# A causal mask added in 64-row halves, and new orders for the attention stage of a fused transformer block

## The chip, the cores and the metric

The kernel runs on one core of a Trainium2 chip. The metric is the device time of one launch in microseconds (us), from runs of the whole program. A profile of one further execution shows every engine: TensorE (PE; its weight loads PEld), VectorE (DVE), ScalarE (ACT), GpSimd (POOL) and SyncE (SP), which issues the transfers.

## The reference

One block on x of shape (8, 512, 256) in float32: a modulated layer norm, causal linear attention with 16 heads of 16, a gated residual, a second modulated layer norm, and a mixture of 8 experts (256 to 1024 to 256, two chosen for each token). Cut to the attention, where the change is:

```python
h = _layernorm(x, axis=-1) * (1 + ca) + sa
qkv = h @ w_qkv                                  # q, k, v: (B, N, 16, 16)
q = elu(rope(q) * SCALE) + 1.0
k = elu(rope(k) * SCALE) + 1.0
def step(carry, qkv_t):
    kv = kv + einsum('bhd,bhm->bhdm', kt, vt)
    ks = ks + kt
    denom = maximum(einsum('bhd,bhd->bh', qt, ks), 1e-06)
    out_t = einsum('bhd,bhdm->bhm', qt, kv) / denom[..., None]
x = x + ga * (out @ w_out)
```

## The kernel before

The 4096 tokens are 32 chunks of 128, four for each of the 8 sequences. The first stage passes over the chunks once. For a chunk it computes the scores k q of all pairs of its 128 tokens, head by head, sets those to zero in which the key is later than the query, multiplies by v, and adds what earlier chunks of the sequence left in a running `state`. The mask is added in PSUM: before the scores, a matmul writes -1e30 at the places of later keys (and 0 elsewhere) into the bank, the scores are accumulated onto it, and a ReLU makes them zero (the true scores are not negative).

Operands are split in a high and a low float16 part. Names in the rows: `st`, `mv`, `var`, `rstd`, `nb` are the layer norm's statistics and factors (two columns, since chunk n's first norm and chunk n-5's second one share them), `h` the normalised rows and, under the same name in the rows, those of the second norm, `hT` the first transposed and modulated, `ra`/`rb` the two products of the rotary embedding, `feat` the features of q and k, `qst`/`kst` their float16 parts stacked for the products, `qstT`/`kstT` those transposed, `amhi`/`amlo` the two parts of the masked scores (a group of 8 heads each, `sc0` and `sc1`), `den` and `attn` the denominator and the quotient, `w1hi`, `w1lo` and `w` the parts of the expert weights, which are prepared in this stage a piece a chunk, `am` (from `wo`) the output projection's weight times the gate, `x` (also `x1`) the rows after the residual.

The order on each engine is written in five tables, `ORDER_PE`, `ORDER_DVE`, `ORDER_POOL`, `ORDER_ACT` and `ORDER_SP`. An entry is a piece of work and its lag: in step n the engine goes through its table and does each piece for chunk n - lag. The engines are tied only by semaphores, so a step begins on each at its own time. Within an engine the order is fixed: a piece that waits holds up everything behind it. The names of the pieces, by engine, with the lines of the function that does them:

- VectorE: `st`, `st2` (L432), `mv`, `mv2` (L438), `ve` (L445, `var`), `f` (L505, `feat`, both inputs in SBUF), `sl0`, `sl1` (L511, `amlo`, one input in PSUM), `nb` (L452, both inputs in SBUF, 2 numbers a partition), `rope` (L495, L498), `x1` (L547), `stl` (L520, `state`; not done for the fourth chunk of a sequence), `hTe` (L475), `wlo` (L558, two instructions, both inputs in SBUF), `den`, `rec`, `vlo`, `at`.
- GpSimd: `shk` (L822), `rs` (L789, `rstd`, needs `ve` and is needed by `nb`), `slo` (L829, L831; needs `shk` and ScalarE's `shq`), `R` (L836, `ra`, needs `rope`), `xm2` and `h2` (both L797), `wb` (L808, `am`, once in four steps).
- TensorE: `sc0`, `sc1` (L1127 the mask, L1135 the scores; `sc1` needs VectorE's `sl0`, `sc0` needs `sl1`), `pj` (L1189 on `am`, `aT`), `aT`, `hT`, `h2T` (L1180), `Tk`, `Tq` (L1172), `v`, `qk` (L1189), `pv0`, `pv1` (L1164 to L1166), `ear` (L1149), `state` (L1235), `lg` (L1263).
- ScalarE: `exp` (L968, L969, needs `R`), `sh0`, `sh1` (L994), `shq` (L932, `qst`), `xn`, `xn2` (L941, need `nb`), `whi`, and the copies out of PSUM (L932).

The score matmuls have 64 rows: the even head of a pair lies on partitions 0 to 63 and goes to bank 5, the odd one on 64 to 127 and goes to bank 6. The mask's matmuls have 128 rows, an identity as weights and the mask, repeated four times, as the 512 columns that pass.

## Time and profile before

| | |
|---|---|
| median of 3 runs | 819.3 us (819.18 to 821.68) |
| profiled execution | 825.53 us, span 823.2 us |
| granted TensorE clock, mean | 0.958 |
| busy: PE, DVE, ACT, POOL | 737.3, 663.8, 580.3, 514.3 us |
| attention stage | about 0 to 380 us of the span |
| routing, then the experts | about 380 to 420, then 420 to 823 us |

Busy times are sums over the span; a matmul's end is modelled, and neighbouring instructions overlap a little. A row's second number is how long its instructions lasted from the first start to the last end; what an instruction holds its engine up by is the distance to the next start.

### The profile page before, as it was taken

The numbers are of one execution on the slowest core, as the hardware profiler recorded it, in microseconds if no ns is written. First come the engines' busy times: TensorE is split into PE (matmuls) and PEld (weight loads), VectorE is DVE, ScalarE is ACT, GpSimd is POOL, SyncE is SP. The second block draws the span as 40 slices with busy tenths as digits, with TensorE's granted clock in tenths as the row PEclk, the third lists the DMA queues.
The fourth block names the chain that finished last, engine by engine and source line by source line (L and its number), as shares of the span: only waits on it lengthen the run. The fifth ranks groups of instructions, "written<-read, shape, count | busy, mean of one in ns | idle before, by whom it ended". The sixth has DMA issues, their size and how long they took to land.

```text
span 823.2 us, 26404 instructions
## 1 busy us (share of the span) xinstructions
PE 737.3 (90%) x7949; PEld 540.3 (66%) x7949; DVE 663.8 (81%) x1488; ACT 580.3 (71%) x1103; POOL 514.3 (62%) x504
## 2 busy tenths in 40 slices
PE   6599999999999999973489999999999999999994
...
GB/s 207 86 41 126 107 115 111 107 108 105 111 113 114 109 116 115 112 53 32 21 79 75 73 71 69 68 78 70 73 73 76 66 69 78 66 76 70 74 31 0
DMA packets 52814, 68.78 MB, mean 84 GB/s; under 512 B 8864, under 2 KB 44080, under 8 KB 52736
## 3 DMA queue, kind: packets, MB, share of 16 engines
...
q14 instruction: 20, 0.16, 0.1%
...
## 4 chain that ended last, share of the span: by engine, by line
PE 59%; DVE 16%; issue 10%; ACT 8%; POOL 3%; DMA 1%; DVEq 1%; another core or an unknown queue 0%; ACTq 0%; SPq 0%; POOLq 0%
PE hidden L1334 15%; PE bank L1350 15%; PE hidden L1336 8%; PE bank L1352 7%; PE bank L1189 5%; PE hidden L1172 3%; DVE amlo L511 2%; DVE nb L452 2%; PE bank L1172 2%; ACT feat L969 2%; ACT rb L968 2%; DVE rb L498 2%; DVE hT L475 2%; DVE st L432 2%; ACT qstT L932 1%
## 5 line engine op out<-in xcount | busy, mean ns | idle before, releaser
L1334 PE MATMUL hidden<-qstT,w1hi_k 128*128 128x256 f16 x1136 | 200.2, 274 | 1.1 <-DVE am L723 1.1
L1336 PE MATMUL hidden<-qstT,w1lo_k 128*128 128x128 f16 x1136 | 195.5, 220 | 0.0
L1350 PE MATMUL bank<-w,amhi 128*128 x568 | 188.6, 379 | 0.4
L1352 PE MATMUL bank<-w,amlo 128*128 x568 | 154.8, 273 | 0.0
L729 DVE TENSOR_TENSOR amlo<-am,amhi 128x512 f16<-128x512 f32 x142 | 98.4, 693 | 62.6 <-ACT am L1064 50.8
L919 POOL DMA_INDIRECT out_dram<-x,si x71 | 121.9, 1717 | 36.5 <-issue 27.4
L1334 PEld LDWEIGHTS hidden<-qstT,w1hi_k 128*128 x1136 | 111.7, 98 | 14.9 <-issue 1.3
L1336 PEld LDWEIGHTS hidden<-qstT,w1lo_k 128*128 x1136 | 111.7, 98 | 1.1
L1189 PE MATMUL bank<-wq,hT 128*128 128x256 f32 (+1 forms) x256 | 102.9, 528 | 9.2 <-DVE hT L475 9.1
L1063 ACT ACTIVATE amhi<-am 128x512 f16<-128x512 f32 x142 | 88.5, 623 | 12.6 <-DVE am L723 7.6
L1350 PEld LDWEIGHTS bank<-w,amhi 128*128 128x128 f16 x568 | 55.5, 98 | 62.3 <-issue 2.6
L1064 ACT ACTIVATE am<-am 128x512 f32<-128x512 f32 x142 | 87.5, 616 | 0.0
L900 POOL DMA_INDIRECT wq<-shares,gi x71 | 67.8, 955 | 22.1 <-issue 14.9
L511 DVE SCALAR_TENSOR_TENSOR amlo<-hidden,amhi 128x1024 f16<-128x1024 f32 x64 | 78.1, 1220 | 2.6 <-ACT amhi L994 2.3
L822 POOL CAST kst<-feat 128x512 f16<-128x512 f32 x32 | 19.5, 609 | 96.9 <-DVE feat L505 96.7
L932 ACT ACTIVATE feat<-hidden 128x512 f32<-128x512 f32 x71 | 42.4, 597 | 40.6 <-PE hidden L1336 36.3
L932 ACT ACTIVATE rb<-hidden 128x512 f32<-128x512 f32 x71 | 42.5, 598 | 38.8 <-PE hidden L1336 37.7
L1189 PEld LDWEIGHTS bank<-wq,hT 128*128 128x128 f32 x256 | 45.6, 198 | 36.3 <-issue 15.9
L994 ACT ACTIVATE amhi<-hidden 128x1024 f16<-128x1024 f32 x64 | 65.0, 1015 | 3.0 <-PE hidden L1135 1.5
L892 POOL DMA_INDIRECT xt<-ffn_rows,gi x36 | 40.4, 1122 | 41.2 <-DVE x L709 38.6
L892 POOL DMA_INDIRECT stage<-ffn_rows,gi x35 | 38.2, 1092 | 42.2 <-DVE x L709 30.7
L1352 PEld LDWEIGHTS bank<-w,amlo 128*128 128x128 f16 x568 | 55.6, 98 | 5.6
...
## 6 DMA issues: line engine op xcount, KB each, us to landing
...
```

The source lines that it names most:

```text
L511: v.scalar_tensor_tensor(out=amlo[:, g, :, :], in0=hidden[1][:, :, :], scalar=0.0, in1=amhi[:, g, :, :], op0=ALU.max, op1=ALU.subtract)\
L729: v.tensor_tensor(glo[:, a.p, h_], g32[:, a.p, h_], ghi[:, a.p, h_], ALU.subtract)\
L892: g.indirect_dma_start(xg[q], None, rows_d, bass.IndirectOffsetOnAxis(ap=gi[:, q, 0:1], axis=0)).then_inc(s_g[q], 16)
L919: g.indirect_dma_start(out_rows, bass.IndirectOffsetOnAxis(ap=si[:, m.c % GB:m.c % GB + 1], axis=0), yw[:, m.p, :], None, bounds_check=T - ...
L932: return v.activation(out_, in_, ACT.Copy, scale=scale)
L1063: v.activation(ghi[:, a.p, h_], g32[:, a.p, h_], ACT.Gelu, scale=1.0 / WS)
L1064: v.activation(g32[:, a.p, h_], g32[:, a.p, h_], ACT.Gelu, scale=1.0 / WS)\
L1189: last = t.matmul(dst, xT_[:, k * P:(k + 1) * P], w[k][:, lo], start=(k == 0), stop=(k == KT - 1))
L1334: t.matmul(dst.rearrange("p (q n) -> p q n", q=2), w1s[0][k][g][:, w_], both, start=(k == 0), stop=False)
L1336: last = t.matmul(dst[:, P:2 * P], w1s[1][k][g][:, w_], both[:, 0, :], start=False, stop=(k == KT - 1))
L1350: t.matmul(y[:, :], ghi[:, m.p, c_m], w2s[mt // 2][:, bass.ds(w_, 2 * D)], start=(mt == 0), stop=False)
L1352: last = t.matmul(y[:, D:2 * D], glo[:, m.p, c_m], w2s[mt // 2][:, bass.ds(w_, D)], start=False, stop=(mt == MT - 1))
```

## The change

Two things are changed. The mask of a bank is added by matmuls of 64 rows instead of 128: for queries 0 to 63 of the chunk and for 64 to 127 apart, with `mask_row` as weights and `later` as what passes, 256 columns each; the odd bank's use partitions 64 to 127. Queries of the first half must not see any key of the second half, which one row of ones times a row of -1e30 says. The constants for it take more instructions on GpSimd. And the five tables are written anew; the lags of `so` (4 to 6) and `ld` (1 to 0) on SyncE change too.

```diff
-ORDER_PE = (("aT", 4), ("ear", 3), ("pj", 4), ("sc1", 3), ("hT", 0), ("pv0", 3), ("Tk", 2), ("h2T", 6), ("v", 0),
-            ("Tq", 2), ("lg", 6), ("pv1", 3), ("state", 2), ("sc0", 2), ("qk", 0))
...
-ORDER_ACT = (("exp", 2), ("sh0", 3), ("shq", 2), ("sth", 3), ("aTe", 4), ("whi", 1), ("xn", 0), ("xn2", 5),
-             ("sh1", 3), ("kTs", 2), ("h2Te", 6), ("vhi", 0), ("qTs", 2), ("lge", 6))
-ORDER_SP = (("ldx", 0), ("ld", 1), ("ro", 6), ("modgb", 6), ("gb", 6), ("modg", 6), ("modb", 7), ("so", 4))
+ORDER_PE = (("aT", 4), ("ear", 3), ("sc1", 3), ("pj", 4), ("hT", 0), ("h2T", 6), ("Tk", 2), ("pv0", 3), ("v", 0),
+            ("Tq", 2), ("pv1", 3), ("lg", 6), ("state", 2), ("sc0", 2), ("qk", 0))
...
+ORDER_ACT = (("exp", 2), ("sh0", 3), ("shq", 2), ("sth", 3), ("aTe", 4), ("xn", 0), ("sh1", 3), ("whi", 1),
+             ("kTs", 2), ("xn2", 5), ("vhi", 0), ("h2Te", 6), ("qTs", 2), ("lge", 6))
+ORDER_SP = (("ldx", 0), ("modg", 6), ("modb", 7), ("so", 6), ("ro", 6), ("ld", 0), ("modgb", 6), ("gb", 6))
...
-        ident_b = sb("ident_b", [P, P], BF16)
-        later = sb("later", [P, P], BF16)
+        mask_row = sb("mask_row", [P, 2, P], BF16)
+        later = sb("later", [P, 2, P // 2], BF16)
...
-        POOL_CONST = 16
+        POOL_CONST = 26
...
+                half = P // 2
+                for u in range(2):
+                    r = slice(u * half, (u + 1) * half)
+                    for late_q in range(2):
+                        link(g.affine_select(out=mask_row[r, late_q, :], in_=mask_row[r, late_q, :],
+                                             compare_op=ALU.not_equal, fill=1.0, base=-half * late_q,
+                                             pattern=[[1, P]], channel_multiplier=-1))
+                    link(g.affine_select(out=later[r, :, :], in_=later[r, :, :], compare_op=ALU.is_ge, fill=MASKED,
+                                         base=0, pattern=[[0, 2], [1, half]], channel_multiplier=-1))
+                    link(g.memset(mask_row[u * half:u * half + 1, 0, 0:half], 0.0))
+                    link(g.memset(mask_row[u * half:u * half + 1, 0, half:P], 1.0))
+                    link(g.memset(later[u * half:u * half + 1, 0, :], MASKED))
...
-                for odd in range(2):
-                    t.matmul(bank[5 + odd].rearrange("p (h t) -> p h t", t=P), ident_b[:, :],
-                             later[:, :].rearrange("p (u t) -> p u t", u=1).broadcast_to([P, 4, P]),
-                             start=True, stop=False, skip_group_check=True)
+                half = P // 2
+                for late_q in range(2):
+                    for odd in range(2):
+                        r = slice(odd * half, (odd + 1) * half)
+                        t.matmul(bank[5 + odd].rearrange("p (h t) -> p h t", t=P)[:, :, late_q * half:(late_q + 1) * half],
+                                 mask_row[r, late_q, :],
+                                 later[r, late_q, :].rearrange("p (u t) -> p u t", u=1).broadcast_to([half, 4, half]),
+                                 start=(late_q == 0), stop=False, skip_group_check=True)
```

The first place is VectorE at the beginning of a step (here the first one whose code is in the loop over sequences), before:

```order
L505 SCALAR_TENSOR_TENSOR feat<-feat,rb 128x512
...
L432 BN_STATS st<-xt 128x6
...
L432 BN_STATS st<-x 128x6
...
L438 BN_AGGR mv<-st 128x2 x2
...
L445 TENSOR_SCALAR var<-mv 128x2
...
L511 SCALAR_TENSOR_TENSOR amlo<-hidden,amhi 128x1024
...
L452 SCALAR_TENSOR_TENSOR nb<-mv,rstd 128x2
```

and now:

```order
L432 BN_STATS st<-x 128x6
...
L432 BN_STATS st<-xt 128x6
L438 BN_AGGR mv<-st 128x2
...
L438 BN_AGGR mv<-st 128x2
...
L445 TENSOR_SCALAR var<-mv 128x2
...
L505 SCALAR_TENSOR_TENSOR feat<-feat,rb 128x512
...
L511 SCALAR_TENSOR_TENSOR amlo<-hidden,amhi 128x1024
...
L452 SCALAR_TENSOR_TENSOR nb<-mv,rstd 128x2
```

`feat` moves from ahead of the statistics to behind `var`, between what `rstd` waits for and the scores. Later in the step `state` now comes before `x`, and `v` before `den`.

The second place is GpSimd in a step in which `am` is made (the seventh step), before:

```order
L822 CAST kst<-feat 128x16x32
L789 TENSOR_TENSOR rstd<-var,minus_half 128x2
L829 TENSOR_TENSOR qst<-feat,qst 128x32x16
L831 TENSOR_TENSOR kst<-feat,kst 128x16x32
L836 TENSOR_TENSOR ra<-ra,rb 128x512
L797 TENSOR_TENSOR h<-h,mod_b 128x256 x2
L808 TENSOR_TENSOR am<-wo,am 128x512
```

and now (the lines are 10 further down in the changed file):

```order
L799 TENSOR_TENSOR rstd<-var,minus_half 128x2
L832 CAST kst<-feat 128x16x32
L839 TENSOR_TENSOR qst<-feat,qst 128x32x16
L841 TENSOR_TENSOR kst<-feat,kst 128x16x32
L818 TENSOR_TENSOR am<-wo,am 128x512
L846 TENSOR_TENSOR ra<-ra,rb 128x512
L807 TENSOR_TENSOR h<-h,mod_b 128x256 x2
```

`rstd` moves ahead of the cast, and `am` from the end to ahead of `ra`.

The third place is TensorE around the second half of the scores, in a step early in the program, before:

```order
L1180 MATMUL bank<-ident,attn 128x128 x2
L1189 MATMUL bank<-am,aT 128x256 x2
L1127 MATMUL hidden<-later,ident_b 128x512 x2
L1135 MATMUL hidden<-qstT,kstT 128x128 x8
L1180 MATMUL bank<-ident,h 128x128 x2
```

and now:

```order
L1194 MATMUL bank<-ident,attn 128x128 x2
L1140 MATMUL hidden<-later,mask_row 128x4x64 x4
L1149 MATMUL hidden<-qstT,kstT 128x128 x8
L1203 MATMUL bank<-am,aT 128x256 x2
L1194 MATMUL bank<-ident,h 128x128 x4
```

The projection (`pj`, on `am` and `aT`) moves behind the scores, and the mask is four matmuls instead of two.

## Rows read from the trace of the kernel before

**Rows 1.** Windows, 100 to 140 us: busy us (instructions) by engine, clock, DMA.

```profile
100.00:140.00 40.00, 36.90 (x505) 25.27 (x501) 38.30 (x85) 34.70 (x64) 25.92 (x28) 1.00 0.36 114
```

**Rows 2.** Source lines L505, L452: duration ns min/median/max, first and last start.

```profile
L505 DVE SCALAR_TENSOR_TENSOR feat<-feat,rb x32: 691/692/694, 27.6 to 353.0; 128x512 f32<-128x512 f32 x32
...
L452 DVE SCALAR_TENSOR_TENSOR nb<-mv,rstd x37: 149/900/1104, 6.4 to 375.2; 128x2 f32<-128x2 f32 x37
```

**Rows 3.** Timeline of VectorE, one step: start, us, instruction [idle before].

```profile
217.50 0.69 DVE L505 SCALAR_TENSOR_TENSOR feat<-feat,rb 128x512 f32<-128x512 f32 x1
...
219.23 0.17 DVE L445 TENSOR_SCALAR var<-mv 128x2 f32<-128x2 f32 x1
219.33 1.23 DVE L511 SCALAR_TENSOR_TENSOR amlo<-hidden,amhi 128x1024 f16<-128x1024 f32 x1
220.47 0.93 DVE L452 SCALAR_TENSOR_TENSOR nb<-mv,rstd 128x2 f32<-128x2 f32 x1
221.33 0.68 DVE L495 TENSOR_TENSOR ra<-bank,cos_t 128x512 f32<-128x512 f32 x1
...
222.86 0.60 DVE L520 TENSOR_TENSOR state<-hidden,state 64x136 f16<-64x136 f32 x2
...
225.26 1.52 DVE L558 SCALAR_TENSOR_TENSOR w<-stage,w 128x512 f32 x2
...
228.13 0.69 DVE L505 SCALAR_TENSOR_TENSOR feat<-feat,rb 128x512 f32<-128x512 f32 x1 [0.16 <-ACT feat L969]
```

**Rows 4.** Timeline of GpSimd, the same step.

```profile
218.53 0.61 POOL L822 CAST kst<-feat 128x512 f16<-128x512 f32 x1 [3.45 <-DVE feat L505]
219.56 0.70 POOL L789 TENSOR_TENSOR rstd<-var,minus_half 128x2 f32<-128x2 f32 x1 [0.42 <-DVE var L445]
220.23 1.16 POOL L829 TENSOR_TENSOR qst<-feat,qst 128x512 f16<-128x512 f32 x1
...
222.68 1.27 POOL L836 TENSOR_TENSOR ra<-ra,rb 128x512 f32<-128x512 f32 x1 [0.18 <-DVE rb L498]
223.91 0.73 POOL L797 TENSOR_TENSOR h<-h,mod_b 128x256 f32<-128x256 f32 x1
224.90 0.73 POOL L797 TENSOR_TENSOR h<-h,mod_b 128x256 f32<-128x256 f32 x1 [0.26 <-POOL h L797]
```

**Rows 5.** Source line L558, 100 to 330 us.

```profile
L558 DVE SCALAR_TENSOR_TENSOR w1lo_k<-stage,w1hi_k x23: 677/683/1220, 109.7 to 329.8; 128x512 f32 x20, 128x512 f16<-128x512 f32 x3
```

**Rows 6.** Timeline of VectorE and GpSimd, another step.

```profile
119.71 1.82 DVE L558 SCALAR_TENSOR_TENSOR w1lo_k<-stage,w1hi_k 128x512 f32 x2
...
119.75 1.23 POOL L797 TENSOR_TENSOR h<-h,mod_b 128x256 f32<-128x256 f32 x1 [0.18 <-POOL h L797]
120.94 1.73 POOL L808 TENSOR_TENSOR am<-wo,am 128x512 f32 x1
```

**Rows 7.** Timeline of TensorE, the step of rows 3.

```profile
220.23 1.13 PE L1189 MATMUL bank<-am,aT 128*128 x4 [0.21 <-ACT aT L932]
221.19 0.59 PE L1127 MATMUL hidden<-later,ident_b 128*128 128x512 bf16 x2
221.72 0.40 PE L1135 MATMUL hidden<-qstT,kstT 64*128 64x128 f16 x8
222.31 0.44 PE L1180 MATMUL bank<-ident,h 128*128 128x128 f32 x2 [0.20 <-ACT h L941]
...
223.20 0.61 PE L1172 MATMUL hidden<-ident,kst 128*128 128x128 f16 x8
```

**Rows 8.** Timeline of ScalarE, the step of rows 3 and the next.

```profile
221.65 0.60 ACT L941 ACTIVATE h<-xt,nb,rstd 128x256 f32 x1 [0.57 <-DVE nb L452]
...
229.00 0.62 ACT L932 ACTIVATE qst<-feat 128x512 f16<-128x512 f32 x1
```

**Rows 9.** Timeline of GpSimd at the start.

```profile
6.34 0.20 POOL L752 MEMSET ones<- 128x128 f16 x1
...
14.99 0.70 POOL L789 TENSOR_TENSOR rstd<-var,minus_half 128x2 f32<-128x2 f32 x1 [3.82 <-DVE var L445]
```

More of the change, by code:

```diff
@@ L58 @@
 Q_SCALE = WS * float(HD ** -0.25)
-ORDER_PE = (("aT", 4), ("ear", 3), ("pj", 4), ("sc1", 3), ("hT", 0), ("pv0", 3), ("Tk", 2), ("h2T", 6), ("v", 0),
-            ("Tq", 2), ("lg", 6), ("pv1", 3), ("state", 2), ("sc0", 2), ("qk", 0))
-ORDER_DVE = (("f", 2), ("st", 0), ("st2", 5), ("mv", 0), ("mv2", 5), ("ve", 0), ("sl0", 3), ("nb", 0), ("rope", 1),
-             ("x1", 4), ("stl", 3), ("hTe", 0), ("sl1", 3), ("wlo", 1), ("den", 3), ("rec", 3), ("vlo", 0), ("at", 3))
-ORDER_POOL = (("shk", 2), ("rs", 0), ("slo", 2), ("R", 1), ("xm2", 5), ("h2", 5), ("wb", 2))
-ORDER_ACT = (("exp", 2), ("sh0", 3), ("shq", 2), ("sth", 3), ("aTe", 4), ("whi", 1), ("xn", 0), ("xn2", 5),
-             ("sh1", 3), ("kTs", 2), ("h2Te", 6), ("vhi", 0), ("qTs", 2), ("lge", 6))
-ORDER_SP = (("ldx", 0), ("ld", 1), ("ro", 6), ("modgb", 6), ("gb", 6), ("modg", 6), ("modb", 7), ("so", 4))
+ORDER_PE = (("aT", 4), ("ear", 3), ("sc1", 3), ("pj", 4), ("hT", 0), ("h2T", 6), ("Tk", 2), ("pv0", 3), ("v", 0),
+            ("Tq", 2), ("pv1", 3), ("lg", 6), ("state", 2), ("sc0", 2), ("qk", 0))
+ORDER_DVE = (("st2", 5), ("st", 0), ("mv2", 5), ("mv", 0), ("ve", 0), ("f", 2), ("sl0", 3), ("nb", 0), ("rope", 1),
+             ("stl", 3), ("x1", 4), ("hTe", 0), ("sl1", 3), ("wlo", 1), ("vlo", 0), ("den", 3), ("rec", 3), ("at", 3))
+ORDER_POOL = (("rs", 0), ("shk", 2), ("slo", 2), ("wb", 2), ("R", 1), ("xm2", 5), ("h2", 5))
+ORDER_ACT = (("exp", 2), ("sh0", 3), ("shq", 2), ("sth", 3), ("aTe", 4), ("xn", 0), ("sh1", 3), ("whi", 1),
+             ("kTs", 2), ("xn2", 5), ("vhi", 0), ("h2Te", 6), ("qTs", 2), ("lge", 6))
+ORDER_SP = (("ldx", 0), ("modg", 6), ("modb", 7), ("so", 6), ("ro", 6), ("ld", 0), ("modgb", 6), ("gb", 6))
 NORM2 = 5
@@ L384, in carry @@
             eng.sem_inc(s_carry, 1)
-        POOL_CONST = 16
-        POOL_TWO, POOL_EROW = 37, 50
+        POOL_CONST = 26
+        POOL_TWO, POOL_EROW = 47, 60
         POOL_IDENT, POOL_FIRST = 2, 4
@@ L753, in attention_constants @@
                 link(g.memset(ident16[:, :], 0.0))
-                link(g.memset(ident_b[:, :], 0.0))
-                link(g.memset(later[:, :], 0.0))
+                link(g.memset(mask_row[:, :, :], 0.0))
+                link(g.memset(later[:, :, :], 0.0))
                 link(g.memset(v16[:, :, 0, :, HD:VW], 1.0))
@@ L758, in attention_constants @@
                 link(g.memset(state[:, :, :, :], 0.0))
-                for t in (ident16, ident_b):
-                    diagonal(t)
-                for t, fill in ((upto, 0.0), (later, MASKED)):
-                    link(g.affine_select(out=t[:, :], in_=t[:, :], compare_op=ALU.is_ge, fill=fill, base=0,
-                                         pattern=[[1, P]], channel_multiplier=-1))
+                diagonal(ident16)
+                link(g.affine_select(out=upto[:, :], in_=upto[:, :], compare_op=ALU.is_ge, fill=0.0, base=0,
+                                     pattern=[[1, P]], channel_multiplier=-1))
[5 more added lines that the diff above has]
+                                             compare_op=ALU.not_equal, fill=1.0, base=-half * late_q,
+                                             pattern=[[1, P]], channel_multiplier=-1))
+                    link(g.affine_select(out=later[r, :, :], in_=later[r, :, :], compare_op=ALU.is_ge, fill=MASKED,
[3 more added lines that the diff above has]
+                    link(g.memset(later[u * half:u * half + 1, 0, :], MASKED))
                 assert link.n == POOL_CONST, link.n
```

## The prediction

> **What bounds the kernel now.** I first read the windows: from 100 to 140 us VectorE is busy 38.3 of 40 us, TensorE 36.9, ScalarE 34.7, GpSimd 25.9, at a granted clock of 1.00 (the level of 2.4 GHz) [rows 1]. Only VectorE has almost no idle time there. The row on `feat` gives the step: 32 starts of L505 from 27.6 to 353.0 us, so 325.4 / 31 = 10.50 us a step [rows 2]. The second stage (from 420 us) and the routing between them are not touched.
>
> Then I read one step of VectorE in order of time, from 217.50 to 228.13, 10.63 us [rows 3]. It is a chain without holes, but `nb` (L452), which works on two numbers a partition, lasts 0.93 us and holds the next start back by 0.86 (220.47 to 221.33). Free, it takes 0.149; its median is 0.900 [rows 2]. GpSimd's `qst` (L829) runs from 220.23 to 221.39 [rows 4]: `nb` ends when that does, at 221.40. The same meeting is seen at L558 (two SBUF inputs too): 0.677 us at best, 1.220 at most [rows 5]. In [rows 6] the pair of L558 takes 1.82 instead of 1.36 and the GpSimd addition beside it 1.23 instead of 0.73: first the addition waits for the first piece, then the second piece for the addition. Operations of VectorE with an input in PSUM show nothing of this: GpSimd's next one, `kst` (L831), fills the time to 222.50 (the row of `ra` at 222.68 has only 0.18 us idle ahead of it [rows 4]), and L495 starts at 221.33 and takes 0.68 beside it [rows 3].
>
> So VectorE's own work in this step is 10.63 less 0.71 (`nb`), 0.16 (L558: 1.52 for 1.36) and 0.16 (`feat` waited for ScalarE) = 9.60 us. What keeps it at 10.5 is mainly the meeting of `nb` with `qst`. TensorE has some 0.8 us of idle time a step (3.1 of 40 us), ScalarE 1.4: both become bounds not far below 9.6.
>
> The Trainium skill (SBUF — State Buffer, Who interferes with whom) says that a VectorE instruction with two SBUF inputs contends with a GpSimd instruction that reads SBUF, that who comes first holds the pair of ports for the whole instruction, and that the order of issue decides who blocks. The rows above agree (0.93 against 0.149). By that rule a new order moves waits rather than removing them; where to, the next part works out from rows.
>
> **The new order, step by step.** I take 0 as the start of VectorE's first statistics in a step, and keep the distances between starts of [rows 3].
>
> VectorE: four statistics and `var` come first now; in [rows 3] `var` is 1.73 behind `feat`, of which `feat` is 0.61, so `var` stands at 1.12. `feat` starts at about 1.20 and ends at 1.89; the scores (L511) start at 1.81 and end at 3.04; `nb` comes up at 2.95 (L511 keeps the next start back 1.14).
>
> GpSimd: `rstd` now stands ahead of `kst`'s cast. It could start 0.16 behind `var`, at 1.45, but `feat` holds the reads to 1.89. In [rows 6] an addition of 0.73 ends 0.59 after the piece that blocked it, so 0.14 of an operation is ahead of the lock; `rstd` (0.70, [rows 4]) ends at 1.89 + 0.56 = 2.45. The cast runs 2.42 to 3.03. `nb` comes up at 2.95: it waits under 0.1 us for the cast. ScalarE's `qst` copy (0.62, 0.18 behind `feat`'s end: 228.82 to 229.00 [rows 8]) is done about 2.7, so L829 starts near 3.0, when `nb` already stands in line. **`nb` costs 0.05 to 0.2 instead of 0.86: 0.7 us saved**, in each of the steps.
>
> Behind it GpSimd has `qst` 3.0 to 4.16, `kst` (1.11 behind it now, 221.39 to 222.50) to 5.28, then `ra` (L836) to 6.5, the multiplication of `h` (L797) 6.5 to 7.2, the addition 7.46 to 8.2: starts at the distances of [rows 4]. The weights' low part (L558) is on VectorE 7.76 behind `feat` now [rows 3]; with `nb` 0.7 shorter and the same work ahead of it, it comes up at 7.05. Its first piece waits for the multiplication's end (to 7.2, of which 0.14 is start-up: nothing), runs to 7.8; the addition has stood in line since 7.46, takes its turn to 8.35; the second piece, up at 7.75, waits and ends near 8.9. Free, it would end at 8.4. **The lock costs 0.5 us there, where it costs 0.16 in the step of rows 3**. So the step is 9.60 + 0.05 + 0.45 = 10.1 us.
>
> In one step of four `am` (L808, 1.73 us [rows 6]) is made. It moves from behind `h` to ahead of `ra`. The same step has no `state` (L520, 0.60 [rows 3]), so L558 is 0.6 earlier. It meets `ra` (1.27): its second piece waits some 1.1 us. That step: 9.60 - 0.6 + 1.2 = 10.2. `ra` is done at 8.7; the next `feat` stands at 10.1 + 1.2 = 11.3, and between them are two operations of ScalarE of about the size of its `qst` copy, so `feat` doesn't wait. The routing constants and `am` also stand ahead of `ra` once at the start: under 1 us.
>
> **The mask.** Before, two matmuls of 512 columns over 128 rows: the first scores start 0.53 after the mask, 221.19 to 221.72 [rows 7]. Of this two streams of 0.213 are columns; about 0.1 is the change to matmuls of 64 rows. After, four of 256 columns over 64 rows each, odd and even in turns. Eight matmuls of 128 columns over 128 rows (L1172) take 0.61 from first start to last end, the eight of the scores, over 64 rows, 0.40 [rows 7]: 30 ns less for each of seven distances, of which the columns are 53 ns at 2.4 GHz. So halves run in pairs, and the mask's four should take 0.21 instead of 0.43; the bounds are nothing saved (they don't pair) and 0.32 (the switch vanishes too). I take 0.22, twice a step. The switch stands ahead of the mask now, and there are as many. The Trainium skill (TensorEngine Tiling, Key Properties) says that tiles work independently and that changing the mode drains the engine; by it the sum would be the same.
>
> These 0.44 us a step are on no bound: TensorE has idle time. They matter in one place. `sc1` now comes before `pj`, and `x` (L547) needs `pj`. From the end of the scores' subtraction: old mask 0.53, scores 0.33, `pj` 1.13 [rows 7] and 0.1 of latency = 2.1 us; VectorE meanwhile does `nb`, rope and `state`: 0.1, 1.53 (221.33 to 222.86, less 0.33 for `x`, which stands there now) and 0.6 [rows 3], about 1.95. With the old mask `x` would wait 0.1 us, and 0.7 in the step without `state`: 0.25 on average. The new mask takes this off nearly whole, so I count 0. `hT`, behind `pj` (0.96 between starts, then 0.44), is ready at about 5.0; L475 comes up at 3.1 + 1.53 + 0.6 = 5.2, behind rope, `state` and `x`; ScalarE's `h` follows `nb` by 0.25 as now (221.40 to 221.65 [rows 8]) and is no later than `pj`.
>
> **The start.** GpSimd's constants run from 6.34 to 11.17 (`rstd` at 14.99 has 3.82 us idle ahead of it [rows 9]), 12 instructions at 0.4 us in the mean. Ten more, net, mostly smaller, are about 3 us and at most 4: they end at 14.2 to 15.2, in the hole or 0.2 beyond it.
>
> **Queues.** SyncE now loads a weight piece a step earlier relative to its use and stores `x1` two steps later, behind waits of its own; a load of `xt` or of a piece has about a step between its issue and its use. I count nothing; were that cover gone, a late one would hold VectorE or ScalarE up by what it lacks, which no row here shows.
>
> **Sum.** Now 10.50 a step; then (3 x 10.1 + 10.2) / 4 = 10.12. Saved 0.38 x 31 = 11.8, less 0.5 for the start: 11.3 us. The profiled execution would go from 825.5 to 814.2, the median of runs from 819.3 to **808.0** (the profiled one is 6.2 above it).
>
> **Rivals.**
> A. The meeting at L558 doesn't happen, because GpSimd's addition falls before or behind it. For: in most steps now it doesn't (half the L558 take under 0.683 [rows 5]), and the new order may settle so. Against: by my times they overlap by half a microsecond. The step is 9.7, a saving of 0.8 x 31 = 25: 794 us. Chance 0.16.
> B. No change: the lock's price at L558 and small waits for `pj`, `hT` or ScalarE come to 0.8 us a step instead of 0.45. For: TensorE and ScalarE have only 0.8 and 1.4 us. Against: the mask gives TensorE 0.44. 817 to 822 us. Chance 0.13.
> C. Slower: L558 meets both the multiplication and the addition in full, each 0.59 of lock: 1.18, so 9.7 + 1.18 = 10.88, 0.38 x 31 = 12 more: 831 us. It decides from 0.8 us of waiting a step on. For: VectorE and GpSimd are tied by their waits, so the meeting, once there, repeats in each step, as `nb`'s does now. Against: it needs L558 0.6 us earlier than I have it. Chance 0.11.
> The forecast itself (L558 loses 0.3 to 0.7 us): 0.60, 801 to 815.
>
> **Range and chances.** About 0.3% is what a measurement can tell from no change, 816.8 to 821.8. Faster: forecast and A, 0.76; same: 0.13; slower: 0.11. For 8 in 10 I take 795 to 821: it leaves out C and the lower half of A.
>
> **What would show it.** Right: `nb` near 0.2 to 0.3 us in the median; L558's mean above 0.9; starts of `feat` 10.1 us apart; the scores 0.3 us behind the mask's first matmul; VectorE again with no idle time. Wrong: `nb` still 0.9 (`feat` or the cast come late, then `qst` is ahead of `nb` again); VectorE waiting for `pj` or for scores (then TensorE's order is the bound); or L558's mean unchanged (A) or above 1.2 (C).

## The result and the profile after

The changed kernel takes 811.5 us (median of 4 executions, 809.99 to 811.72); the kernel before, on the same chip, takes 820.5 us (4 executions, 819.18 to 821.68). The ratio is 0.989, with a 95% interval of 0.986 to 0.991: 9.0 us less by the medians, where 11.3 were forecast. The time lies within the forecast's own 801 to 815. One execution is left out of all that follows, of the run e6 below: it took 3306 us, the other five 805.1 to 807.7.

The profiled execution took 809.99 us, its span is 807.9. The same stretch of windows as in [rows 1], columns as there:

```profile
100.00:140.00 40.00, 36.02 (x533) 27.89 (x529) 36.98 (x86) 35.81 (x67) 28.91 (x29) 1.00 0.39 120
```

VectorE (third figure) has gone from 38.3 to 37.0 busy us of 40 although more operations fit in: it now has 3.0 us of idle time. ScalarE has 35.8 instead of 34.7. The clock is at its upper level, as before. The source lines of `feat`, `nb` and the low parts (L558; these from 100 to 330 us), to be held against [rows 2, 5] (duration ns min/median/max, first and last start):

```profile
L505 DVE SCALAR_TENSOR_TENSOR feat<-feat,rb x32: 683/685/793, 28.7 to 341.9; 128x512 f32<-128x512 f32 x32
L452 DVE SCALAR_TENSOR_TENSOR nb<-mv,rstd x37: 147/150/1129, 6.4 to 364.5; 128x2 f32<-128x2 f32 x37
L558 DVE SCALAR_TENSOR_TENSOR w1lo_k<-stage,w1hi_k x24: 679/948/1420, 107.7 to 319.6; 128x512 f32 x20, 128x512 f16<-128x512 f32 x4
L558 DVE SCALAR_TENSOR_TENSOR w<-stage,w x22: 678/681/685, 128.1 to 329.5; 128x512 f32 x18, 128x512 f16<-128x512 f32 x4
```

[rows 5] has the pieces of L558 that write `w1lo_k`; those that write `w` took, before:

```profile
L558 DVE SCALAR_TENSOR_TENSOR w<-stage,w x21: 676/680/1150, 99.9 to 310.1; 128x512 f32 x19, 128x512 f16<-128x512 f32 x2
```

From the first `feat` to the last it is now 341.9 - 28.7 = 313.2 us, 10.10 a step, against 325.4 and 10.50 [rows 2]: 12.2 us saved there, 11.8 were forecast. The first `feat` starts 1.1 us later, which leaves 11.1 at the last one. Behind the last `feat` the two profiled executions differ by another 4 us (span less last start: 470.2 and 466.0), 3.5 of it in the experts: from the first start of L729 to the last it is 386.3 and 382.7 us. The change doesn't touch that stage, and of the runs below e10 to e12 take 385.8 to 386.5 there and the others 382.3 to 382.9, whatever their orders: that belongs to the executions. `nb` is at 0.150 in the median instead of 0.900.

VectorE, one step and the end of the next:

```profile
222.16 0.41 DVE L438 BATCH_NORM_AGGREGATE mv<-st 128x2 f32<-128x6 f32 x2
222.78 0.17 DVE L445 TENSOR_SCALAR var<-mv 128x2 f32<-128x2 f32 x1 [0.21 <-DVE mv L438]
222.86 0.68 DVE L505 SCALAR_TENSOR_TENSOR feat<-feat,rb 128x512 f32<-128x512 f32 x1
223.46 1.22 DVE L511 SCALAR_TENSOR_TENSOR amlo<-hidden,amhi 128x1024 f16<-128x1024 f32 x1
224.59 0.15 DVE L452 SCALAR_TENSOR_TENSOR nb<-mv,rstd 128x2 f32<-128x2 f32 x1
224.66 0.68 DVE L495 TENSOR_TENSOR ra<-bank,cos_t 128x512 f32<-128x512 f32 x1
225.26 0.68 DVE L498 TENSOR_TENSOR rb<-bank,sin_t 128x512 f32<-128x512 f32 x1
225.86 0.60 DVE L520 TENSOR_TENSOR state<-hidden,state 64x136 f16<-64x136 f32 x2
226.70 0.42 DVE L547 TENSOR_TENSOR x<-bank,xt 128x256 f32<-128x256 f32 x1 [0.24 <-PE bank L1203]
227.04 0.72 DVE L475 TENSOR_SCALAR hT<-bank,mod_t 128x128 f32<-128x128 f32 x2
227.68 1.21 DVE L511 SCALAR_TENSOR_TENSOR amlo<-hidden,amhi 128x1024 f16<-128x1024 f32 x1
228.81 1.28 DVE L558 SCALAR_TENSOR_TENSOR w1lo_k<-stage,w1hi_k 128x512 f32 x2
...
232.62 0.68 DVE L505 SCALAR_TENSOR_TENSOR feat<-feat,rb 128x512 f32<-128x512 f32 x1
...
236.52 0.42 DVE L547 TENSOR_TENSOR x<-bank,xt 128x256 f32<-128x256 f32 x1 [0.82 <-PE bank L1203]
...
238.63 2.37 DVE L558 SCALAR_TENSOR_TENSOR w1lo_k<-stage,w1hi_k 128x512 f32 x2
```

GpSimd, the same two steps:

```profile
223.11 0.99 POOL L799 TENSOR_TENSOR rstd<-var,minus_half 128x2 f32<-128x2 f32 x1 [1.11 <-DVE var L445]
224.05 0.61 POOL L832 CAST kst<-feat 128x512 f16<-128x512 f32 x1
224.81 1.16 POOL L839 TENSOR_TENSOR qst<-feat,qst 128x512 f16<-128x512 f32 x1 [0.15 <-POOL kst L832]
...
229.73 0.96 POOL L807 TENSOR_TENSOR h<-h,mod_b 128x256 f32<-128x256 f32 x1 [1.39 <-ACT h L951]
...
236.82 1.27 POOL L818 TENSOR_TENSOR am<-wo,am 128x512 f32 x1
238.04 1.28 POOL L846 TENSOR_TENSOR ra<-ra,rb 128x512 f32<-128x512 f32 x1
239.28 1.18 POOL L807 TENSOR_TENSOR h<-h,mod_b 128x256 f32<-128x256 f32 x1
```

Read them side by side. `nb` (224.59) is done before `qst` starts (224.81): the order of the two has turned round, as forecast. `rstd` starts at 223.11, while `feat` holds the reads, and takes 0.99 instead of 0.70. The low parts (228.81) run free at 1.28, since the multiplication of `h` now comes behind their start, at 229.73: it waited 1.39 for ScalarE's `h`. In the step with `am`, `ra` comes late (238.04) and the pair takes 2.37. And `x` (L547), which never waited in [rows 3], waits for the projection's matmuls, 0.24 us here and 0.82 in the step without `state`. A second new wait, 0.21 us ahead of `var` (L445), is put down to VectorE's own `mv`; it comes in three steps of four, and what causes it was not tried.

TensorE, at the second scores of this step, for [rows 7]:

```profile
224.73 0.39 PE L1140 MATMUL hidden<-later,mask_row 64*128 64x256 bf16 x4 [0.32 <-DVE amlo L511]
224.96 0.39 PE L1149 MATMUL hidden<-qstT,kstT 64*128 64x128 f16 x8
225.28 1.13 PE L1203 MATMUL bank<-am,aT 128*128 x4
```

From the mask's first matmul to the first scores it is 0.23 us, where it was 0.53. `pj` starts 0.55 behind the mask and `x` 1.42 behind `pj`. So the path is: scores' subtraction ends (224.68), mask, scores, `pj`, `x`.

### The profile page after: what moved, and what is told of

Same layout as the page of the kernel before. It is cut to its first block, busy times and chain, and to the rows that moved or that the text cites. A ratio compares the mean times of both kernels' runs of the same rounds, so it can differ in the third digit from the quotient of the medians.

```text
span 807.9 us, 26660 instructions
## 1 busy us (share of the span) xinstructions
PE 716.7 (89%) x8077; PEld 548.9 (68%) x8077; DVE 642.3 (80%) x1488; ACT 573.0 (71%) x1103; POOL 540.8 (67%) x514
## 4 chain that ended last, share of the span: by engine, by line
PE 54%; DVE 20%; issue 12%; POOL 8%; ACT 2%; DVEq 1%; DMA 1%; POOLq 0%; SPq 0%; ACTq 0%
PE hidden L1348 16%; PE bank L1364 15%; PE hidden L1350 8%; PE bank L1366 7%; DVE amlo L511 3%; PE bank L1203 3%; DVE w1lo_k L558 2%; PE bank L1186 2%; DVE st L432 1%; DVE hT L475 1%; POOL mod_b L880 1%; DVE rb L498 1%; POOL rstd L799 1%; POOL qst L839 1%; POOL kst L841 1%
## 5 line engine op out<-in xcount | busy, mean ns | idle before, releaser
L1348 PE MATMUL hidden<-qstT,w1hi_k 128*128 128x256 f16 x1136 | 198.1, 273 | 0.0
L929 POOL DMA_INDIRECT out_dram<-x,si x71 | 129.2, 1820 | 38.3 <-issue 22.1
L729 DVE TENSOR_TENSOR amlo<-am,amhi 128x512 f16<-128x512 f32 x142 | 98.3, 692 | 51.3 <-ACT am L1074 48.2
L807 POOL TENSOR_TENSOR h<-h,mod_b 128x256 f32<-128x256 f32 x64 | 59.7, 933 | 42.7 <-ACT h L951 36.1
L910 POOL DMA_INDIRECT wq<-shares,gi x71 | 68.2, 961 | 22.1 <-DMA out_dram<-x,si 14.6
L799 POOL TENSOR_TENSOR rstd<-var,minus_half 128x2 f32<-128x2 f32 x37 | 35.8, 968 | 66.2 <-DVE var L445 66.1
L511 DVE SCALAR_TENSOR_TENSOR amlo<-hidden,amhi 128x1024 f16<-128x1024 f32 x64 | 77.8, 1216 | 1.0 <-ACT amhi L1004 0.7
L723 DVE TENSOR_TENSOR am<-hidden,rb 128x512 f32<-128x512 f32 x71 | 49.1, 691 | 29.0 <-ACT rb L942 28.9
```

What stands on the lines that cost most here:

```text
L511: v.scalar_tensor_tensor(out=amlo[:, g, :, :], in0=hidden[1][:, :, :], scalar=0.0, in1=amhi[:, g, :, :], op0=ALU.max, op1=ALU.subtract)\
L729: v.tensor_tensor(glo[:, a.p, h_], g32[:, a.p, h_], ghi[:, a.p, h_], ALU.subtract)\
L929: g.indirect_dma_start(out_rows, bass.IndirectOffsetOnAxis(ap=si[:, m.c % GB:m.c % GB + 1], axis=0), yw[:, m.p, :], None, bounds_check=T - ...
L1348: t.matmul(dst.rearrange("p (q n) -> p q n", q=2), w1s[0][k][g][:, w_], both, start=(k == 0), stop=False)
```

## The experiments

Two theories stood at the start, called L and M in the expectations. L is the prediction's: the orders free `nb` and bring the gain, the mask's matmuls are on no bound. M: the faster mask made the gain, the orders little. What the runs left standing is neither: what `nb` gives back comes again as other waits, and the mask's time is on the path of one of them. Every ratio is to the kernel before on the same chip; its medians were 821.1, 820.6, 825.6 and 822.0 us in the four sets (e1 to e4; e5 to e9; e10 to e12; e13). "Step" is the mean distance of the 32 starts of `feat`.

### The change taken apart: e1_old_mask and e2_mask_only

e1 has all the new orders and the old mask:

```diff
-                        t.matmul(bank[5 + odd].rearrange("p (h t) -> p h t", t=P)[:, :, late_q * half:(late_q + 1) * half],
-                                 mask_row[r, late_q, :],
...
+                    t.matmul(bank[5 + odd].rearrange("p (h t) -> p h t", t=P), ident_b[:, :],
+                             later[:, :].rearrange("p (u t) -> p u t", u=1).broadcast_to([P, 4, P]),
+                             start=True, stop=False, skip_group_check=True)
```

Expected: 

> The kernel before with the five new order tables and the old mask (two matmuls of 512 columns over 128 rows). Theory L (the gain is the meeting of nb with a GpSimd read that is gone): VectorE's nb again takes 0.15 us, and nearly all of the gain is there; only x waits longer for pj behind the slower mask, up to 0.3 us a step, so 812 to 818 us, ratio 0.990 to 0.998. Theory M (the faster mask made the gain, the orders little): 819 to 822 us, ratio 1.00, although nb takes 0.15.

Measured: 824.5 us, ratio 1.004 (1.002 to 1.005); step 10.52. VectorE and TensorE of e1:

```profile
222.12 0.15 DVE L452 SCALAR_TENSOR_TENSOR nb<-mv,rstd 128x2 f32<-128x2 f32 x1
...
224.67 0.42 DVE L547 TENSOR_TENSOR x<-bank,xt 128x256 f32<-128x256 f32 x1 [0.68 <-PE bank L1189]
...
226.85 1.82 DVE L558 SCALAR_TENSOR_TENSOR w<-stage,w 128x512 f32 x2
```

```profile
222.27 0.60 PE L1127 MATMUL hidden<-later,ident_b 128*128 128x512 bf16 x2 [1.00 <-DVE amlo L511]
222.80 0.40 PE L1135 MATMUL hidden<-qstT,kstT 64*128 64x128 f16 x8
223.13 1.13 PE L1189 MATMUL bank<-am,aT 128*128 x4
```

`nb` is free here too, and nothing is gained: L's 812 to 818 us is missed, and the time is a little above M's 819 to 822. Mask to scores is 0.53, mask to `pj` 0.86, which is 0.31 more than after, and `x` waits 0.57, 0.67, 0.56 and 1.15 us in the four kinds of step instead of 0.24, 0.35, 0.24 and 0.82: 0.33 more in each. Being later, the low parts meet GpSimd's `h` again (1.82 instead of 1.28) in two steps of four.

e2 has the new mask in the old orders (the diff of e1 the other way round, on the kernel before).

Expected: 

> The kernel before with the new mask alone (four matmuls of 256 columns over 64 rows), the old orders. Theory L: TensorE has idle time and VectorE doesn't, so nothing: 819 to 821 us, ratio 0.998 to 1.001, nb's median still 0.9 us, the distance from the mask's first matmul to the scores 0.23 us instead of 0.53. Theory M: 0.6 us less on TensorE in each of 32 steps is most of the gain: 811 to 815 us.

Measured: 822.8 us, ratio 1.002 (1.000 to 1.003); step 10.48, `nb` still 0.9. TensorE is busy 35.2 of 40 us from 100 to 140 us instead of 36.9: the time is off TensorE, but it was nobody's wait. That is against M, which asked for 811 to 815. So neither part brings anything alone, and the two together bring 1.1%.

### One wait removed by two moves: e3_two_swaps

The kernel before, with `f` behind `ve` and `rs` ahead of `shk`:

```diff
-ORDER_DVE = (("f", 2), ("st", 0), ("st2", 5), ("mv", 0), ("mv2", 5), ("ve", 0), ("sl0", 3), ("nb", 0), ("rope", 1),
+ORDER_DVE = (("st", 0), ("st2", 5), ("mv", 0), ("mv2", 5), ("ve", 0), ("f", 2), ("sl0", 3), ("nb", 0), ("rope", 1),
-ORDER_POOL = (("shk", 2), ("rs", 0), ("slo", 2), ("R", 1), ("xm2", 5), ("h2", 5), ("wb", 2))
+ORDER_POOL = (("rs", 0), ("shk", 2), ("slo", 2), ("R", 1), ("xm2", 5), ("h2", 5), ("wb", 2))
```

Expected: 

> The kernel before (old mask) with two moves alone: feat (f) behind var on VectorE, rstd (rs) ahead of the cast (shk) on GpSimd. Theory L: these two moves are what frees nb; its median falls from 0.9 to 0.15 us, and the step from 10.5 to 9.9 to 10.2 us, so 808 to 815 us, unless feat, now 1.2 us later, makes the scores' operands late. Theory M or a theory that the other moves matter as much: 818 us or more.

Measured: 825.2 us, ratio 1.004 (1.003 to 1.006); step 10.51. `nb` takes 0.15. ScalarE, TensorE and VectorE of e3:

```profile
228.40 0.63 ACT L932 ACTIVATE qst<-feat 128x512 f16<-128x512 f32 x1 [0.68 <-DVE feat L505]
228.94 0.57 ACT L932 ACTIVATE state<-hidden 64x136 f16<-64x136 f32 x2
229.53 0.38 ACT L932 ACTIVATE aT<-bank 128x256 f32<-128x256 f32 x1
```

```profile
229.97 1.13 PE L1189 MATMUL bank<-am,aT 128*128 x4 [0.78 <-ACT aT L932]
```

```profile
231.39 0.42 DVE L547 TENSOR_TENSOR x<-bank,xt 128x256 f32<-128x256 f32 x1 [0.61 <-PE bank L1189]
```

The wait has moved: `feat` is later, ScalarE's `qst` copy waits for it (0.68), `aT` stands behind that in ScalarE's order, `pj` waits for `aT` (0.78) and `x` for `pj` (0.61). The 0.7 us of `nb` went to `x`, which waits 0.62, 0.87 and 0.62 us in three kinds of step; in the one with `am`, `hT` waits 0.56 for TensorE. The 808 to 815 us expected are missed: these two moves free `nb` and are no gain without others.

### The lock by itself: e4_nb_one_input

The kernel before with `nb` written as two instructions that have one tensor input in SBUF each; `rstd` comes in as the scalar of each partition. Same values, same orders, old mask.

```diff
-                v.scalar_tensor_tensor(out=nb[:, :], in0=mv[:, :, 0], scalar=-1.0, in1=rstd[:, :],
-                                       op0=ALU.mult, op1=ALU.mult).then_inc(a_["nb"], 1)
+                for k in range(2):
+                    last = v.tensor_scalar(nb[:, k:k + 1], mv[:, k, 0:1], rstd[:, k:k + 1], -1.0, ALU.mult, ALU.mult)
+                last.then_inc(a_["nb"], 1)
```

Expected: 

> The kernel before with the same orders and mask, but nb is made by two instructions of one column each, which have one tensor input (mv) and take rstd as a scalar for each partition, instead of one with two SBUF tensor inputs. Theory L in its strict form (what blocks is the second SBUF tensor input): the two take 0.15 us each and start without waiting for GpSimd's qst, 0.25 us for the pair instead of 0.86, a saving of 0.6 us a step, 804 to 812 us (ratio about 0.985). Rival: any VectorE instruction that starts beside a GpSimd one on small tensors, or the wait for rstd, is what holds it up: nb still ends when qst does, 819 to 824 us.

Measured: 807.6 us, ratio 0.983 (0.981 to 0.985); step 9.98. GpSimd and VectorE of e4:

```profile
220.30 1.17 POOL L830 TENSOR_TENSOR qst<-feat,qst 128x512 f16<-128x512 f32 x1
```

```profile
220.51 0.33 DVE L453 TENSOR_SCALAR nb<-mv,rstd 128x1 f32<-128x1 f32 x2
220.75 0.68 DVE L496 TENSOR_TENSOR ra<-bank,cos_t 128x512 f32<-128x512 f32 x1
...
224.69 1.82 DVE L559 SCALAR_TENSOR_TENSOR w1lo_k<-stage,w1hi_k 128x512 f32 x2
```

`nb` stands in the middle of `qst`, exactly where it took 0.9, and takes 0.33 for both columns. That shows the cause of its 0.9: the second tensor input in SBUF, not its place as such. The instruction's kind, which e4 changes too, is not it: L511 is a SCALAR_TENSOR_TENSOR with one input in PSUM, and in [rows 3] it takes 1.23 us beside GpSimd's `rstd` (219.56), where its mean is 1.22. The Trainium skill (SBUF — State Buffer, Who interferes with whom) says that a VectorE instruction with at most one SBUF input, outside the modes in which it uses both ports, doesn't contend with GpSimd; this run agrees (0.33 for the two, in the middle of `qst`). Part of what `nb` gave back was lost at L559 (L558 before), whose pair takes 1.82 in most steps where it took about 1.5. And this edit of three lines gains more than the change does.

### The mask's order: e5_no_pairs

The changed kernel with the two loops of the mask exchanged, so that a row group's two matmuls follow each other:

```diff
-                for late_q in range(2):
-                    for odd in range(2):
+                for odd in range(2):
+                    for late_q in range(2):
```

Expected: 

> The changed kernel, with the mask's four matmuls in another order: both of the even bank (rows 0 to 63), then both of the odd bank, so that neighbours use the same rows of the array. If matmuls on different rows run in pairs, this undoes the pairing: the first scores start 0.4 to 0.45 us behind the mask's first matmul instead of 0.23, and since the old mask on these orders cost 1.5% at 0.53, this costs about two thirds of that: 818 to 822 us. If the pairing is not what shortened the mask (but that no change of row mode lies between mask and scores), it stays at 0.23 to 0.3 and 811 us.

Measured: 812.7 us, ratio 0.990 (0.988 to 0.992); step 10.12. TensorE of e5:

```profile
225.28 0.40 PE L1140 MATMUL hidden<-later,mask_row 64*128 64x256 bf16 x4 [0.32 <-DVE amlo L511]
225.50 0.39 PE L1149 MATMUL hidden<-qstT,kstT 64*128 64x128 f16 x8
225.82 1.13 PE L1203 MATMUL bank<-am,aT 128*128 x4
```

0.22 to the scores and 0.54 to `pj`: as after. The order within the mask doesn't matter. The 818 to 822 us expected of matmuls that can no longer pair are missed. But they still pair: mask and scores are 4 x 256 + 8 x 128 = 2048 columns in 0.54 us, which one behind the other at the rate of the wide ones (0.213 us for 512, as in the prediction) would take 0.85; and of the mask's four, two start within 0.01 us of each other and the other two, as close together, 0.12 later, in e5 as after. Which row group each of them belongs to, the trace doesn't tell.

### Where `am` is made: e6_wb_last and e12_old_mask_wb_last

The changed kernel with `wb` back at the end of GpSimd's order:

```diff
-ORDER_POOL = (("rs", 0), ("shk", 2), ("slo", 2), ("wb", 2), ("R", 1), ("xm2", 5), ("h2", 5))
+ORDER_POOL = (("rs", 0), ("shk", 2), ("slo", 2), ("R", 1), ("xm2", 5), ("h2", 5), ("wb", 2))
```

Expected: 

> The changed kernel with GpSimd's am (wb) back behind h (h2), as before the change. In the changed kernel the one step in four with am takes 10.65 us and the others 9.9 in the mean, with L558 at 2.37 us in it and 1.28 in the others. If am's place is the cause, that step falls to 9.8 to 10.1, since am then lies in GpSimd's idle time behind h: 8 steps x 0.6 = 5 us less, 805 to 808 us. Rival: am then is in the way of the next step's rstd (idle before it now: 1.1 us, am takes 1.3 to 1.7), nb and all behind it come 0.5 us late: 810 to 813 us.

Measured: 807.1 us, ratio 0.982 (0.980 to 0.984); step 9.91. Its low parts (L558), 100 to 330 us:

```profile
L558 DVE SCALAR_TENSOR_TENSOR w1lo_k<-stage,w1hi_k x24: 678/682/687, 105.2 to 312.8; 128x512 f32 x20, 128x512 f16<-128x512 f32 x4
```

The longest is 0.687 us, against 1.420 after. The step with `am` takes 9.97 instead of 10.65; the waits of `x` are as after. So `am` ahead of `ra` costs the change 0.68 us in each fourth step, 0.17 a step, 5 us in all, as expected.

e12 is e6 with the old mask (the diff of e1 on it).

Expected: 

> The new orders with am (wb) behind h (the run that gave 807.1 us with the new mask), and the old mask. If the old mask costs on these orders because x, behind pj, behind the scores, is 0.33 us later in every step and L558 with it, it costs here what it cost with am where the change has it, 0.3 to 0.5 us a step: 817 to 823 us. If it was the meeting with am that the old mask made worse, 808 to 812 us.

Measured: 825.8 us, ratio 1.001 (0.999 to 1.003); step 10.45. `x` waits 0.56, 0.67, 0.56 and 1.15, the low parts take 1.82 in three steps of four. On these orders the mask is worth 0.55 us a step. By the ratio (the kernel before takes 825.6 us in this set) that is the first branch of the expectation, what the old mask cost with `am` in its new place.

### Taking `x`'s wait away: e8_pj_early

The changed kernel with `pj` ahead of `sc1` again, and `aTe` ahead of `shq` and `sth` on ScalarE:

```diff
-ORDER_PE = (("aT", 4), ("ear", 3), ("sc1", 3), ("pj", 4), ("hT", 0), ...
+ORDER_PE = (("aT", 4), ("ear", 3), ("pj", 4), ("sc1", 3), ("hT", 0), ...
-ORDER_ACT = (("exp", 2), ("sh0", 3), ("shq", 2), ("sth", 3), ("aTe", 4), ("xn", 0), ...
+ORDER_ACT = (("exp", 2), ("sh0", 3), ("aTe", 4), ("shq", 2), ("sth", 3), ("xn", 0), ...
```

Expected: 

> The changed kernel with pj back ahead of sc1 on TensorE, and the copy it needs (aTe) ahead of shq and sth on ScalarE. VectorE's x waits 0.24 to 0.82 us a step for pj in the changed kernel. If that wait is on the path that sets the step, it goes and the step falls by 0.2 to 0.4: 801 to 808 us. Rival: what counts is how soon the scores follow VectorE's amlo, and pj ahead of them makes them up to 0.5 us late: 812 to 820 us.

Measured: 815.1 us, ratio 0.993 (0.992 to 0.995); step 10.27 (10.01, 9.91, 10.11 and 10.93 with `am`). `x` waits no more than 0.1 us, and the kernel is slower than the changed one. The 801 to 808 us expected are missed; the time is the rival's, but VectorE's `amlo` never waits for late scores. VectorE and GpSimd of e8 in the step with `am`:

```profile
233.78 0.69 DVE L505 SCALAR_TENSOR_TENSOR feat<-feat,rb 128x512 f32<-128x512 f32 x1
...
239.49 2.94 DVE L558 SCALAR_TENSOR_TENSOR w1lo_k<-stage,w1hi_k 128x512 f32 x2
```

```profile
236.01 1.16 POOL L839 TENSOR_TENSOR qst<-feat,qst 128x512 f16<-128x512 f32 x1 [0.42 <-ACT qst L942]
...
239.48 1.27 POOL L846 TENSOR_TENSOR ra<-ra,rb 128x512 f32<-128x512 f32 x1
```

VectorE comes to L558 5.71 us behind `feat`, 0.30 earlier than after (6.01). GpSimd comes to `ra` at 5.70, 0.28 later than after (5.42), since ScalarE now copies `aT` ahead of `qst`, for which GpSimd waits 0.42. Together that is the 0.57 by which the pair is longer (2.94 against 2.37): it meets all of `ra`. `hT` waits 0.34 for TensorE in this step besides. In the other three steps L558 is free, and yet none is shorter than after (10.02, 9.92, 9.76): there `den` waits 0.12 to 0.18 us for TensorE's product, and `v` 0.25 for ScalarE's copy in the one of 10.11. What `x` gave back, the lock took in one step of four and other waits in the rest.

### The mask beside the free `nb`: e9_nb_and_mask

The kernel before, with the edit of e4 and the new mask, old orders.

Expected: 

> The orders of before, with nb in two instructions of one SBUF tensor input each and the new mask. With the old mask this nb gave 807.6 us, a step of 9.98 us, TensorE busy 38.8 of 40 us. If TensorE's chain is a bound beside VectorE's there, the mask's 0.6 us a step are worth something now, down to VectorE's own work of about 9.7: 799 to 805 us. If VectorE alone is the bound (L558 meets h's addition in each step, 1.82 for 1.28), the mask is worth nothing, as it was with the old nb: 807 to 809 us.

Measured: 806.7 us, ratio 0.982 (0.980 to 0.984); step 9.93. Against e4's 0.983 that is within what can be told, and nearest to the expectation's second branch, VectorE alone as the bound. `x` doesn't wait in the attention steps of it, but for the last few: `pj` stands ahead of the mask in the old order, so the mask isn't on `x`'s path.

### Which move frees the low parts: e10_late_xn2, e11_xn2_wb_mid, e13_later_xn2

By the rows after, L558 is free in the changed kernel because ScalarE's `xn2` (its `h` of the second norm) is later. e10 is e9 with that move alone:

```diff
-ORDER_ACT = (("exp", 2), ("sh0", 3), ("shq", 2), ("sth", 3), ("aTe", 4), ("whi", 1), ("xn", 0), ("xn2", 5),
-             ("sh1", 3), ("kTs", 2), ("h2Te", 6), ("vhi", 0), ("qTs", 2), ("lge", 6))
+ORDER_ACT = (("exp", 2), ("sh0", 3), ("shq", 2), ("sth", 3), ("aTe", 4), ("whi", 1), ("xn", 0),
+             ("sh1", 3), ("kTs", 2), ("xn2", 5), ("h2Te", 6), ("vhi", 0), ("qTs", 2), ("lge", 6))
```

e11 adds `wb` between `R` and `xm2` on GpSimd; e13 is e11 with `xn2` behind `vhi`:

```diff
-             ("sh1", 3), ("kTs", 2), ("xn2", 5), ("h2Te", 6), ("vhi", 0), ("qTs", 2), ("lge", 6))
+             ("sh1", 3), ("kTs", 2), ("h2Te", 6), ("vhi", 0), ("xn2", 5), ("qTs", 2), ("lge", 6))
```

Expected of e10: 

> The orders of before, the new mask, nb in two instructions of one SBUF tensor input (as in the run that gave 806.7 us), and ScalarE's xn2 moved from behind xn to behind kTs. In that run L558 takes 1.82 us in each step because GpSimd's addition to h reads SBUF beside it. With xn2 some 2 us later, GpSimd's multiplication and addition to h lie mostly behind L558, as in the changed kernel. If each meeting of a two-input VectorE instruction with a GpSimd read costs its lock time, L558 falls to 1.28 and the step from 9.93 to 9.4 to 9.6 us: 790 to 798 us. Rival: VectorE's own work or another engine (ScalarE 36.5 of 40 us busy) already holds the step at 9.9, or GpSimd's cast for the next step comes late behind h: 803 to 808 us.

Measured: 816.0 us, ratio 0.989 (0.987 to 0.991); step 10.09. The low parts still take 1.81 in three steps of four: VectorE comes to L558 at 225.95 and the multiplication of `h` to GpSimd at 226.47, that is in the middle of the pair:

```profile
226.47 0.75 POOL L808 TENSOR_TENSOR h<-h,mod_b 128x256 f32<-128x256 f32 x1 [1.40 <-ACT h L952]
227.48 0.88 POOL L808 TENSOR_TENSOR h<-h,mod_b 128x256 f32<-128x256 f32 x1 [0.26 <-POOL h L808]
```

After, it comes 0.92 us behind the pair's start and the pair is free; here it comes 0.52 behind it and takes its turn between the pieces. 0.4 us decide, and `xn2` alone brings none of the gain. The 790 to 798 us expected are missed, and e10 is even slower than e9 (10.09 a step for 9.93): `am`, behind `h`, is later too and meets the next step's `feat`, which waits out part of it:

```profile
238.59 1.24 DVE L506 SCALAR_TENSOR_TENSOR feat<-feat,rb 128x512 f32<-128x512 f32 x1
```

```profile
238.01 1.27 POOL L819 TENSOR_TENSOR am<-wo,am 128x512 f32 x1
```

In the step with `am`, `den` waits 1.05 for TensorE besides.

Expected of e11: 

> As e10_late_xn2, with GpSimd's am (wb) between ra (R) and h (xm2), where GpSimd would wait for xn2. It then reads SBUF beside L558 in one step of four and makes that step's L558 0.8 to 1.1 us longer: 2 us more than e10_late_xn2 over 8 steps if am behind h costs the cast nothing, 2 us less if am behind h makes the next step's cast and rstd late.

Measured: 814.1 us, ratio 0.987 (0.985 to 0.989); step 10.00; the low parts 1.82, and 2.62 with `am`. The 2 us less than e10 are the expectation's second branch: `feat` no longer meets `am`.

Expected of e13: 

> As e11_xn2_wb_mid, with ScalarE's xn2 another two places later, behind vhi and ahead of qTs. In e10_late_xn2 the multiplication of h still began 0.5 us behind L558's start and L558 took 1.81 us. Now xn2 ends some 0.9 us later, so that multiplication and addition come behind L558. If L558 then takes 1.28 us in three steps of four and this wait is what sets the step, it falls from 10.0 to 9.5 us: ratio 0.970 to 0.977, better than all kernels so far. Rival: qTs, 0.5 us later behind xn2, makes the scores late, or TensorE and ScalarE hold the step: ratio 0.982 to 0.990 although L558 is free.

Measured: 814.0 us, ratio 0.991 (0.989 to 0.992); step 10.20. The low parts are free (1.28) in most steps, and still it is longer; VectorE of e13 shows why:

```profile
221.05 0.69 DVE L506 SCALAR_TENSOR_TENSOR feat<-feat,rb 128x512 f32<-128x512 f32 x1 [0.47 <-ACT feat L980]
```

`xn2` stands ahead of `qTs` now and holds up ScalarE's chain to `feat`; `den` waits 0.35 for TensorE besides. The gain at L558 has turned into these waits, as the expectation's rival had it (its ratio ended at 0.990, and 0.991 was measured).

### The table

| orders | old mask: ratio, step us | new mask: ratio, step us |
|---|---|---|
| before | 1, 10.50 | 1.002, 10.48 |
| before, `nb` with one SBUF tensor (e4, e9) | 0.983, 9.98 | 0.982, 9.93 |
| new (e1, the change) | 1.004, 10.52 | 0.989, 10.10 |
| new, `am` last (e12, e6) | 1.001, 10.45 | 0.982, 9.91 |

The mask is worth nothing on the old orders, where `pj` stands ahead of the second scores, and 1.5 to 1.9% on the new ones, where it stands behind them. That it is `pj`'s place and no other difference of the orders is read from the waits of `x` (0.33 us more in each step of e1); the new orders with `pj` ahead and the old mask were not tried. Nor were the other moves of the five tables and SyncE's lags by themselves.

## Why the prediction was right, point by point

**What bounds the kernel, and `nb`.** Right: VectorE's chain set the step, and the meeting of `nb` with `qst` kept it at 10.5; e4 takes only that away and gets 9.98. In the step of the kind of [rows 3] it takes 10.12 (`feat` at 207.45 and 217.57). My 9.60 holds 0.15 for `nb`, which costs 0.24 there, and 1.36 for L558, which takes 1.81: 10.14. That `rstd` would be held by `feat` and end about 2.45 is what the rows show (223.11 + 0.99 = 224.10, 2.60 behind the first statistics at 221.50). `nb` was to cost 0.05 to 0.2; it costs 0.07.

**L558 in the common step.** Wrong: it was to lose 0.5 us and loses nothing. I had the multiplication of `h` follow `ra` at once. In fact it waits 1.39 for ScalarE's `h`, whose place (`xn2` behind `kTs`) I had not worked out, and comes 0.9 behind L558's start. That is rival A's mechanism. The mean of L558 is 0.787 us (36.2 us in 46 pieces from 100 to 330 us), before it was 0.789: not above 0.9, as "what would show it" asked, but unchanged, the sign of A. The mean hides that three steps of four went from about 1.5 to 1.28 and the fourth from 1.82 to 2.37. I had misread [rows 5] here as well: a median of 0.683 doesn't mean that most steps had no meeting, since only one piece of a pair is held; before, every pair from the fourth step on takes 1.42 or more. And a free pair is 1.28, not the 1.36 that I counted.

**`x` and the mask.** Wrong in the attribution. I counted nothing, since the new mask would take the wait off nearly whole; VectorE waiting for `pj` stood among the signs of being wrong. The four waits of `x` are 0.24, 0.35, 0.24 and 0.82, 0.41 a step in the mean, and they take the place of the 0.45 that I had put on L558. Two terms were off. From `pj`'s last matmul (225.28 + 1.13 = 226.41) to `x` it is 0.29 us, where I took 0.1 of latency; and VectorE's work in between is 1.78 (224.68 to 226.46), not 1.95. That I gave the mask "on no bound" in one sentence and took 0.25 us a step off by it in another was the weak place: e1 and e12 show that it carries the whole gain of these orders, 0.42 and 0.55 us a step, where I had 0.25, since the later `x` also brings L558 back into its meeting.

**The mask's size.** The mask to the scores went from 0.53 to 0.23 us: 0.30, near the upper bound of 0.32, not the 0.22 taken. So the switch to 64 rows, some 0.1 us by my estimate, has left this place as well. The Trainium skill (TensorEngine Tiling (Array Packing), Key Properties) says that a change of mode drains TensorE; the 0.1 us fits that. If the switch stands ahead of the mask now, it lies in a stretch where TensorE waits for VectorE anyway (0.32 us): the mask starts 0.05 us behind the end of `amlo`, and 0.06 in e1 with the old mask.

**The step with `am`.** The place was right: L558's pair meets `ra` and takes 2.37, which is 1.09 above the free 1.28 (1.1 were forecast). The step is 10.65 and not 10.2, since `x` waits 0.82 in it; the other three take 9.90 in the mean and not 10.1.

**The start.** Right: GpSimd's constants end at 14.20, as said, in its idle time ahead of `rstd` (14.89); the first `feat` is 1.1 us later, a little above the bound of 1 us (0.5 were counted), with statistics now ahead of it.

**Queues.** Right: no engine waits for a transfer from 60 to 345 us, before or after.

**The sum.** 10.12 a step forecast, 10.10 measured. Two errors of nearly the same size and of opposite sign (0.45 at L558 in three steps of four, 0.41 at `x`) made it come out: that the time is right is luck in this part. Of the signs named, `nb`, the step and the scores' distance came as forecast; L558's mean did not, and VectorE has 3.0 us of idle time in 40, where none was forecast. The forecast was right on the time and on `nb`, and wrong on what takes back a part of it. Of the 11.1 us that the traces show at the last `feat`, the medians show 9.0; the interval of the ratio, times 820.5, reaches from 7.3 to 11.2 us. What the rest is, if it is more than scatter, was not tried. One thing that the traces show bears on it, and on every experiment: what is gained by the last `feat` isn't all kept. From there to the first L729 of the experts it is 69.9 us before, 69.4 after, and 70.2 to 74.4 in the twelve other runs, and TensorE's clock is at its lower level (0.50, that is 1.2 GHz) for 47.8, 51.2 and, in e6, 68.2 us of it. In e6 it fell at 336.3 us (TensorE was busy 6.0 of the 8 us from 328 to 336), before at 371.3; e6 is 18.1 us ahead at the last `feat`, and its ratio is worth 14.5. In e2, whose step is like before, the stretch takes 73.5. Why the clock falls earlier was not tried.
